# Gated cross-attention and expert block on one core: tokens' columns laid out by partition in DRAM, three groups of TensorE work placed later

## What is computed

```python
x = x + tanh(g_xattn[0]) * xattn(layernorm(x), ctx)   # 32 heads, 8 kv heads of 128, rmsnorm on q and k, softmax
x = x + tanh(g_ffn[0]) * ffn(layernorm(x))
# ffn: scores = xf @ Wr.T; the 16 best of 64 experts; gates = softmax of those scores
#      h = einsum('nd,krd->nkr', xf, A); out = einsum('nkr,kdr->nd', h * G[:, :, None], B) * 2
```

## Time and profile before

| | us |
|---|---|
| median of 3 runs | 2317.74 (2317.13 to 2318.9) |
| the profiled execution's own time | 2318.4 |
| its span, first to last instruction | 2316.6 |
| TensorE busy | 2261.6 (98%) |
| VectorE busy | 1597.6 (69%) |
| ScalarE busy | 1183.9 (51%) |
| GpSimd busy | 1144.8 (49%) |
| mean share of the 16 DMA engines, hardware queue q1 | 44.1% |

### The profile page before, as it was taken

How to read it: one execution, slowest core, us unless ns; L and a number is a source line. 1 busy time by engine, 2 the same in 40 slices (tenths; PEclk the granted TensorE clock), 3 DMA queues, 4 the chain that set the end, 5 groups by cost and what they waited for, 6 DMA issues and landing times.

```text
span 2316.6 us, 35630 instructions
## 1 busy us (share of the span) xinstructions
PE 2261.6 (98%) x11615; PEld 1906.0 (82%) x11615; DVE 1597.6 (69%) x2669; ACT 1183.9 (51%) x3773; POOL 1144.8 (49%) x1735
## 2 busy tenths in 40 slices
PE   6999999999999999999999999999999999999999
PEld 5887887888888878888888788888888887888787
DVE  7558558777777797777777954755756878555755
ACT  5546546666666676666666732422424335333421
POOL 3666566666555555555555453233232664534221
PEclk9999999999999999999999999999999999999999
DMA  5688466767667367764322635645557566323643
GB/s 198 218 245 296 150 197 232 212 165 204 183 170 191 121 212 205 230 179 128 110 91 92 209 100 164 182 127 166 162 152 216 186 217 255 128 92 136 237 164 136
DMA packets 177062, 408.78 MB, mean 176 GB/s; under 512 B 11824, under 2 KB 77616, under 8 KB 159664
## 3 DMA queue, kind: packets, MB, share of 16 engines
q1 hardware_dynamic: 169392, 351.97, 44.1%
q0 software_dynamic: 7488, 54.53, 12.9%
HBM read 282.72 MB, written 190.84 MB: 204 GB/s over the span
## 4 chain that ended last, share of the span: by engine, by line
PE 84%; DVE 4%; POOL 4%; issue 3%; ACT 3%; DMA 2%; SPq 0%; POOLq 0%; ACTq 0%; DVEq 0%
PE bank L769 23%; PE bank L771 23%; PE bank L770 23%; PE bank L827 4%; PE bank L835 2%; PE bank L815 2%; DVE t_lo L1320 1%; PE bank L852 1%; PE bank L851 1%; PE bank L850 1%; ACT t_hi L1024 1%; POOL s_hi L1811 1%; DVE s_lo L1320 1%; DMA t_raw<-combos 1%; DMA staged<-in_w_q 1%
## 5 line engine op out<-in xcount | busy, mean ns | idle before, releaser
L769 PE MATMUL bank<-t_hi,s_hi 128*128 128x512 f32 x2688 | 1084.0, 403 | 30.7 <-DVE t_lo L1320 17.3
L771 PE MATMUL bank<-t_hi,s_lo 128*128 128x512 f32 x2688 | 1053.8, 392 | 0.0
L770 PE MATMUL bank<-t_lo,s_hi 128*128 128x512 f32 x2688 | 1050.9, 391 | 0.0
L769 PEld LDWEIGHTS bank<-t_hi,s_hi 128*128 128x128 f32 x2688 | 507.2, 189 | 128.1 <-issue 32.3
L771 PEld LDWEIGHTS bank<-t_hi,s_lo 128*128 128x128 f32 x2688 | 505.8, 188 | 110.7
L1320 DVE TENSOR_TENSOR s_lo<-staged,s_hi 128x512 fp32r<-128x512 f32 x672 | 525.0, 826 | 88.9 <-ACT s_hi L1035 86.9
L770 PEld LDWEIGHTS bank<-t_lo,s_hi 128*128 128x128 f32 x2688 | 507.5, 189 | 90.3
L1035 ACT CAST s_hi<-staged 128x512 fp32r<-128x512 f32 x434 | 250.2, 623 | 184.9 <-POOL staged L1801 71.5
L1782 POOL TENSOR_SCALAR small<-small 128x4 f32<-128x4 f32 (+1 forms) x192 | 75.9, 395 | 446.9 <-ACT small L1131 341.4
L1799 POOL TENSOR_TENSOR staged<-staged 128x512 f32<-128x512 f32 x86 | 115.3, 1340 | 365.5 <-DMA staged<-heads 196.9
L1463 DVE SCALAR_TENSOR_TENSOR probs<-bank,small,mask 128x128 f32<-128x128 f32 x512 | 143.9, 343 | 87.1 <-POOL small L1789 43.6
(11 more groups left out here) (143 smaller groups left out, 2894.7 us busy)
## 6 DMA issues: line engine op xcount, KB each, us to landing
heads<-heads SPq DMA_DIRECT2D x128, 256.0 KB, 4.3
staged<-in_w_q SPq DMA_DIRECT2D x32, 768.0 KB, 5.2
staged<-heads SPq DMA_DIRECT2D x32, 768.0 KB, 6.9
sums<-sums POOLq DMA_DIRECT2D x24, 1024.0 KB, 8.0
t_raw<-in_sets SPq DMA_DIRECT2D x20, 1024.0 KB, 7.1
t_raw<-combos SPq DMA_DIRECT2D x19, 1024.0 KB, 8.6
xt<-x_columns SPq DMA_DIRECT2D x8, 1792.0 KB, 6.8
combos<-in_sets POOLq DMA_DIRECT2D x14, 1024.0 KB, 10.2
```

The costliest lines, as they stand in the source:

```text
L769: nc.tensor.matmul(out, s_hi[w][:, cols], high, start=start, stop=False, skip_group_check=True)
L770: nc.tensor.matmul(out, s_hi[w][:, cols], low, start=False, stop=False, skip_group_check=True)
L771: done = nc.tensor.matmul(out, s_lo[w][:, cols], high, start=False, stop=at == 3, skip_group_check=True)
```

## The change

Five edits. The scratch `xt` is laid out [2, 7, 128, 4, 512] in place of [2, 7, 4, 128, 512], so a partition's four pieces of 2 KB are one run of 8 KB when it is read, and lie 8 KB apart between partitions when it is written. In e8 and e9 the first four key transposes and the first four token transposes of an entry stand after beat 3 instead of 2. In e80 alone the router stands after beat 4 instead of 3, its scores' transposes after beat 5, its copy-out at beat 5, and `choose` part 0 at beat 6, behind the next entry's first two s low parts. The last pair's gating steps count from e89 instead of e88. In `y_rows`, result 21 is no longer formed and then added: `usum` is added at beat 5 by a new instruction, and the bank itself at beat 7.

```diff
@@ -186,7 +186,7 @@
-        self.xt = scratch("xt", 2, 7, 4, P, HALF)
+        self.xt = scratch("xt", 2, 7, P, 4, HALF)
@@ -314,7 +314,7 @@
-    ct = [m.over(name, [P, HALF], rw_at + w * HALF * 4) for w, name in enumerate(("c22", "c12", "c21"))]
+    ct = [m.over(name, [P, HALF], rw_at + w * HALF * 4) for w, name in enumerate(("c22", "c12"))]
@@ -371,10 +371,14 @@
+    def router_beat(e):
+        return 4 if e == A0 else 3
+
     def tiles_at(beat, table):
         found = []
         for i in range(PAIRS):
-            at = beat - plan.beat0[A0 + i + 1]
+            at = beat - plan.beat0[A0 + i + (2 if i == PAIRS - 1 else 1)]
             found += [(i, t) for t in table.get(at, ())]
@@ -467,7 +471,7 @@ refill
-                src = d.xt[tau - 2, k].rearrange("a p c -> p a c")
+                src = d.xt[tau - 2, k]
@@ -479,7 +483,7 @@ load_first_ahead
-                src = d.xt[0, 0].rearrange("a p c -> p a c")
+                src = d.xt[0, 0]
@@ -553,7 +557,7 @@ columns_out
-            sp.dma_start(d.xt[u // 4, :, u % 4].rearrange("k p c -> p k c"), xo[:, :, :, :].rearrange("p k b q -> p k (b q)")).then_inc(xt_out, 16)
+            sp.dma_start(d.xt[u // 4, :, :, u % 4].rearrange("k p c -> p k c"), xo[:, :, :, :].rearrange("p k b q -> p k (b q)")).then_inc(xt_out, 16)
@@ -637,7 +641,9 @@ y_rows_out
             sp.wait_ge(y_set, 3 * i + 2 + w)
-            if w == 0:
+            if w:
+                sp.wait_ge(taken[3], plan.after[B0 + i, 6])
+            else:
                 sp.wait_ge(taken[0], plan.after[B0 + i, 4])
@@ -929,7 +935,7 @@ TensorE, e0 to e15
-                if e and j == 2:
+                if e and j == (3 if e in (8, 9) else 2):
                     key_columns(e - 1, 0)
                     x_columns(e - 1, 0)
@@ -969,9 +975,9 @@ TensorE, e80 to e87
                 rank_columns(plan.beat0[e] + j)
-                if j == 3:
+                if j == router_beat(e):
                     router(e - A0)
-                if j == 4:
+                if j == router_beat(e) + 1:
                     score_rows(e - A0)
@@ -1294,8 +1300,9 @@ ScalarE, e80 to e87
+                if j == router_beat(e) + 1:
+                    router_scores(e - A0)
                 if j == 4:
-                    router_scores(e - A0)
                     rank_tile(e - A0)
@@ -1595,10 +1602,11 @@ y_rows, beat 5 and beat 7
                 nc.vector.scalar_tensor_tensor(yr[b][0][:, right], ct[1][:, :], tg2[:, :], yr[b][0][:, right], ALU.mult, ALU.add).then_inc(y_set, 1)
+                nc.vector.scalar_tensor_tensor(yr[b][1][:, left], usum[:, :], tg2[:, :], yr[b][1][:, left], ALU.mult, ALU.add).then_inc(y_set, 1)
             if j == 7:
-                result21(e, ct[2][:, :])
-                dve.wait_ge(taken[3], plan.after[e, 6])
-                nc.vector.scalar_tensor_tensor(yr[b][1][:, left], ct[2][:, :], tg2[:, :], yr[b][1][:, left], ALU.mult, ALU.add).then_inc(y_set, 1)
+                dve.wait_ge(prod, plan.prod[e, 6])
+                dve.wait_ge(y_set, 3 * i + 3)
+                nc.vector.scalar_tensor_tensor(yr[b][1][:, left], bank[3][:, :], tg2[:, :], yr[b][1][:, left], ALU.mult, ALU.add).then_inc(taken[3], 1)
@@ -1745,6 +1753,7 @@ VectorE, e80 to e87
                 if j == 5:
                     rank_tile(i, 2)
+                if j == router_beat(e) + 2:
                     choose(i, 0)
```

## The result

| | before | after |
|---|---|---|
| median of 16 runs each, us | 2318.39 (2317.13 to 2319.29) | 2322.03 (2319.57 to 2322.89) |
| ratio, 95% interval | | 1.0015 (1.0008 to 1.0021) |
| the profiled execution's own time | 2318.4 | 2319.57 |
| its span | 2316.6 | 2317.7 |

The change makes the kernel slower by 3.6 us (by the interval, 1.9 to 4.9). The time is 2.6 us above the 2319.4 that was named. It is inside the range of 2315.0 to 2322.2, but only 0.2 us from its upper end, and just outside the 2322.0 of the likeliest case's own range; that it still falls inside is in part luck. The sign of the sum was right.

The account below looks back on a forecast made before the run. TensorE, busy 98% of the span, was taken as the bound, with VectorE setting some entries' ends. Terms summed to +1.7 us on 2318.4, so 2320.1, less 0.66 for the runs' median: 2319.4 us, range 2315.0 to 2322.2.

Parts of the forecast that it names:

- e89: Entry 89 of the trace: transposes +0.36 us, new instruction +0.68, late gates meeting its end +0.2.
- e88: Entry 88 of the trace: two fewer GpSimd gates -0.3 us, the new instruction +0.68, together +0.37.
- e8, keys: Entry 8: moved key transposes gain 0, since VectorE's first s low part still sets the next entry's start.
- e9, keys: Entry 9, where VectorE has slack: TensorE's wait at the key transposes goes, gain 1.9 us (1.7 to 2.1).
- e80 and e81, router: Moving the router in entry 80 lets the next entry start earlier, gain 0.93 us (0 to 1.0).
- e90: Entry 90: four transposes +0.47 us, late gating's store competing with a load +0.5, new instruction +0.5.
- e91 to e94: Each next entry starts late behind the new VectorE instruction, 0.48 to 0.68 us each, +2.2 us together.
- behind the last product: At the kernel's end one instruction of 0.75 us stands in place of 0.69 + 0.75 us: -0.72 us.
- (a): The new y instruction costs nothing, absorbed by VectorE's 1.97 us of idle time: 2315.4 us; chance 0.16.
- (b): Every named wait goes, at the keys, the router, the gates and the tail: 2305.5 us; chance 0.06.
- (c): Entry 9's wait is replaced by a low part or the staging load, 1.9 us back: 2321.3 us; chance 0.10.
- (d): Pauses at ends of entries 89 to 94 bring half-clock stretches; two add 3.4 us, 2322.8 us; chance 0.08.

Follow-up runs that it names:

- e16: Not a run: a stretch (entry) of the kernel's trace; 29.58 us in the changed kernel's first profile, 29.98 in its second.
- e35: Not a run: an entry of the kernel's trace, 29.31 to 30.61 us over the fourteen profiles.
- e33: Not a run: an entry of the kernel's trace, 30.08 us in the second profile of the kernel before, as in the first.
- e32: Not a run: an entry of the kernel's trace; both profiles of the kernel before have a half-clock stretch in it, at 847.3 and 847.6 us.
- after_again: The changed kernel run once more with no edit, for a second profile: 2321.0 us, ratio 1.0012.
- y_only: The kernel before with only the y_rows and y_rows_out edits: 2322.12 us, ratio 1.0018.
- all_but_y: The changed kernel with y_rows and y_rows_out as before, all other edits kept: 2316.09 us, ratio 0.9992.
- y_late: The changed kernel with the instruction adding usum moved to the end of beat 6, behind the next entry's first s low parts: 2316.13 us, ratio 0.9991.
- e95: Not a run: a late entry of the kernel's trace; from its start to the end 23.84 us before the change, 23.26 after.
- all_but_gating: The changed kernel with the last pair's gating put back where it was: 2318.07 us, ratio 0.9999.
- layout_only: The kernel before with only the new layout of xt: 2317.89 us, ratio 1.0001.
- e48: Not a run: an entry of the kernel's trace; the layout-only profile has a half-clock stretch in it, with the next entry at 25.06 us against 23.72.

## Why the prediction was right, and where it missed

Term by term, the sum against the first profiles of the two kernels:

| term | forecast | measured |
|---|---|---|
| layout | 0 | 0 (ratio 1.0001) |
| e8, keys | 0 | 0.0 |
| e9, keys | -1.9 | -1.96 |
| e80 and e81, router | -0.93 | -0.79 |
| e88 | +0.37 | +0.36 |
| e89 | +1.24 | +1.06 |
| e90 | +1.47 | +1.78 |
| e91 to e94 | +2.2 | +2.31 |
| behind the last product | -0.72 | -0.58 |
| sum | +1.7 | +2.2 |

The rest, 1.1 us between +2.2 and the spans' +1.1, is mostly in e16 to e35, which no edit touches but the layout's: e33 lost 0.77 (the half-clock stretch in e32 that it didn't have), e35 lost 0.48, e17 0.24, and e16 grew by 0.6.

The router's -0.79, and the -1.2 of the edit alone, both hold something else. In e80 ScalarE waits for a load of the new set, which lands now earlier, now later, and the third t high part and t low part wait with it. These are its rows in the first profile of before and in `after_again`, and the one in the first profile of after:

```profile
1957.47 1.91 ACT L1024 CAST t_hi<-t_raw 128x2048 fp32r<-128x2048 f32 x1 [0.73 <-DMA t_raw<-combos]
...
1955.01 1.91 ACT L1030 CAST t_hi<-t_raw 128x2048 fp32r<-128x2048 f32 x1 [0.74 <-DMA t_raw<-combos]
...
1954.57 1.91 ACT L1030 CAST t_hi<-t_raw 128x2048 fp32r<-128x2048 f32 x1 [0.88 <-DMA t_raw<-combos]
```

Pairs with the same wait compare like with like. At 0.73 and 0.74 us, e80 and e81 take 53.65 us before and 52.72 after. At 0.42 us in `y_only` they take 53.41, at 0.43 in `all_but_y` 52.45. The edit is worth 0.93 and 0.96, which is the term of the forecast.

**Right.** The account of what bounds each stretch held. *The keys*: e8's end stands at VectorE's first s low part, e9 is seamless. *The router*: TensorE waits 1.79 us before product 4 for the t low part and 1.11 us for the token rows, the two that the prediction counted through. *The y rows*: the slack of 0.2 us is all there was, and an instruction of 0.74 us costs 0.5 to 0.7 each time. `y_late` shows that its place is the cause: the same instruction behind the s low parts leaves e91 to e94 as they were before. Rivals (a) and (b) fall with that. Rival (c) falls too: nothing takes the place of e9's wait. Of the signs named for a wrong forecast none came: e91 to e94 did not stay at 19.1, e8 did not get shorter, and the granted clock of e89 to e95 stayed at 1.00 in both profiles of the changed kernel.

**Mis-sized, e90.** The forecast took +0.5 for e90's meeting with GpSimd (0 to 0.9). The new instruction itself meets it at the end of e90, GpSimd's last sum L1814 running 1.76 us from 2212.76:

```profile
2212.62 0.75 DVE L1604 SCALAR_TENSOR_TENSOR y_rows<-c,small,y_rows 128x512 f32<-128x512 f32 x1
2213.29 1.78 DVE L1605 SCALAR_TENSOR_TENSOR y_rows<-usum,small,y_rows 128x512 f32<-128x512 f32 x1
2214.99 2.48 DVE L1327 TENSOR_TENSOR s_lo<-staged,s_hi 128x512 fp32r<-128x512 f32 x4
```

L1605 takes 1.78 us instead of 0.74. It ends 0.55 us behind the end of GpSimd's instruction (2214.52). At the end of e89 the pair is a gate that ends at 2193.57 and an L1605 of 1.54 us that ends 0.54 us behind it; in the kernel with the y edit alone, a sum and an L1600 of 1.78 us, 0.55 us apart. That fits VectorE's own work starting when GpSimd's is nearly over. So a meeting costs 1.04 us for this instruction, and 1.1 for four s low parts (below), above the 0.9 that the prediction took as its most. By the Trainium skill (SBUF — State Buffer, "SBUF: two separate sides") the two exclude each other for whole instructions; these three pairs agree with that. Still, its total of 1 us more did not come, because a meeting at the end of e89 was there before the change: there the four s low parts took 3.58 us instead of 2.48. The late gates took that meeting's place. What a meeting costs must be set against the one that it replaces.

What e90 has above the forecast comes mostly from the gating and not from the new instruction. With the gating alone e90 grows by 1.19 us, where the prediction had 0.97, and with the y edit alone by 0.57; together that is 1.76, and 1.78 was measured. With the gating alone GpSimd's last sum meets the s low parts at that place instead, and the four take 3.59 us in place of 2.48. What moved is the sums: in the five kernels with the gating edit they wait for the load of `staged` and start 14.1 to 14.2 us into e90, in the others 12.6 to 12.7, and on SyncE's queue the store of the gated tiles now stands ahead of that load. So the meeting is there whichever instruction of VectorE stands in the place.

**Where the 2.6 us are.** The weak step is the last one: "its runs have the median 2317.74, 0.66 lower, so I forecast 2319.4". First, 0.65 us: that median was of three runs. Over 16 runs the kernel before has 2318.39, the time of its profiled execution, so there was no offset to take off. Second, 0.5 us: the terms came to +2.2 and not +1.7, e90 above all. Third, 1.4 us: the medians differ by 3.6, the touched entries by 2.2. The prediction let the offset of one execution carry over from one kernel to the other, and it does not: the median of after lies 2.5 and 0.7 us above its two profiled executions, that of before 0.0 and 2.2 us below.

The cause of the third part is open, and it need not be real. The +2.2 lies within the interval of the medians' difference, 1.9 to 4.9 us, and `after_again` gives +2.4 both ways. Two things that differ between executions of one kernel are seen in the profiles, and of neither is it shown that the change makes more: half-clock stretches, and loads that land earlier or later (ahead of e8, in e80).

For the stretches speaks the mean granted clock of the runs of after. The profiled one has 0.999; the other fifteen have 0.998 (five, mean 2321.4 us) and 0.997 (ten, mean 2322.2 us). A stretch of 3.41 us at half clock lowers a mean by 0.0007, so they have one or two stretches more; where these fell has no trace. Against them as the whole cause: the runs of before in the same set as `after_again` take 2317.9 us at 0.998 and 2318.8 at 0.997, those of `after_again` 2320.6 and 2322.0. At the same mean clock the changed kernel is still 2.7 to 3.2 us slower. And in `all_but_gating`, `y_late` and `layout_only` the runs with the lower clock are no slower than the others. So either the stretches of the changed kernel stand in dearer places, or something else adds to it; no run here decides between the two.

Rival (d) wanted two stretches at 1.7 us each, in e89 to e95. In both profiles of the changed kernel none is there, but `y_late`, with the same gating, has one at e89's start behind a pause of 2.89 us, where it goes with 1.5 us. For the runs without a trace (d) is not excluded.

Whether the gating makes a stretch in e89 likelier is not settled. The medians lean to it: the gating costs 2.1 us alone and 2.9 to 4.0 in the change, the entries say 1.4 and 1.6, and the uncertainty of such a difference is about 2. Against it, the kernel with the keys alone has such a stretch in e89 without the gating, behind a pause of 2.44 us; and with the layout alone a pause of 2.42 us in that place was followed by none, and so were 2.3 and 2.2 us in the two profiles of the changed kernel.

## What to carry to other kernels

Ask of each instruction that is moved or added what stands between the wait that its engine has just come out of and the next thing that another engine waits for. An engine that idles for 2 us per entry has no room at all in that place, and behind the four s low parts the same instruction was free. A wait of TensorE in a stretch that VectorE fills is worth less than its length when it goes: nothing in e8, 0.3 us of 2.4 in e88, 0.9 of 2.9 in e80. The one wait whose removal paid in full was in an entry where every other engine had slack. And sum against the profiled execution, but take a second one, and more than three runs, before an offset to the median is used.

## What the runs showed of the hardware

The granted clock drops to half for 3.41 us, or twice that, partly at places that differ between executions of one kernel, and its price depends on the place. In e88, nothing (26.86 us with and without), and in e8 nothing that can be read. In e16, where 13 of the 14 profiles have one, nothing that can be read: e16 and e17 take 54.9 us together in nine of them and in the one without. In e32, 0.8 us in the entry behind it (two profiles), in e48 1.3 us (one). In e80 with the router's pause of 2.9 us: 29.20 and 28.97 without a stretch, 29.57 and 29.43 with 3.41 us, 30.70 and 30.79 with 6.83 us. In e89, 1.5 us (two profiles).

The stretches in e80 and e89 begin close to a pause of 2.4 to 2.9 us, those in e32 and e48 just behind one of 1.0 us. Such a pause is not always followed by one: with the router's pause in e80 it was in four of six executions, and in none of the eight where that pause was 1.8 us. By the rule cited for rival (d) (the Trainium skill, TensorE: Matmul & The Clock Gate, "Part 1: The HAM clock gate") an idle TensorE goes back to half rate; these traces agree in the direction, but not each time. One profile can't tell how often it strikes. So taking a pause away may be worth more than its length, but no median here shows that.

A load can land late in one execution and not in another: ScalarE waits 0.5 to 0.6 us for one ahead of e8 in two profiles, and e8 with e9 is 0.6 to 0.7 us longer in both. In e80 its wait for a load runs from 0.01 to 0.88 us over the fourteen.

A VectorE instruction that meets one of GpSimd's is longer: a `scalar_tensor_tensor` took 1.54 to 1.78 us in place of 0.74, and four s low parts took 3.58 in place of 2.48.
